# A gated-MLP and scan kernel: weights rounded by matmuls in two halves, statistics woven between other operations, prologue queues reordered

## What is computed

```python
x = L0_attn_x                                   # 4 x 1024 x 128, f32
xn = _layernorm(x)                              # over the last axis
x = x + attn(xn, ...) + ffn(xn, w_gate, w_up, w_down)

# attn: causal convolution of xn along time with a complex decaying phasor
#       plus the state carried in, times a gate, real part
# ffn:
def fp4_quant_dequant(x):                       # blocks of 16 along the last axis
    scale = max(max|xb| / 6, 1e-12)
    xn = xb / scale
    q = GRID[searchsorted(MID, |xn|)] * sign(xn) * scale   # grid 0 .5 1 1.5 2 3 4 6
def fp4_linear(x, w):
    return einsum('bsk,nk->bsn', fp4_quant_dequant(x), fp4_quant_dequant(w))
h = silu(fp4_linear(x, w_gate)) * fp4_linear(x, w_up)      # 352 wide
out = fp4_linear(h, w_down)
```

## Time and profile before

| what | us |
|---|---|
| median of 3 runs (range) | 137.78 (137.71 to 139.31) |
| the profiled execution, its own time | 136.63 |
| its span, first to last instruction | 134.8 |

### The profile page before, as it was taken

One profiled execution on the slowest core, in us unless ns is written; L12 is line 12 of the kernel. 1 busy time (PEld: TensorE's weight loads), 2 busy tenths in 40 slices (PEclk: granted clock), 3 DMA queues, 4 the chain that ended last, 5 costly groups with the idle time before them and its releaser, 6 DMA issues.

```text
span 134.8 us, 2143 instructions
## 1 busy us (share of the span) xinstructions
PE 111.7 (83%) x641; PEld 83.7 (62%) x641; DVE 120.6 (89%) x215; ACT 98.7 (73%) x223; POOL 110.4 (82%) x129
## 2 busy tenths in 40 slices
PE   3602789869376999899899999999999999976993
PEld 3501254536243877668786869587868878766882
DVE  0889999999999999979999999999999999899840
ACT  3869966699973899579897889579786648724631
POOL 4568996999699999999999999999999944982220
PEclk9985699986999999999999999999999999999999
DMA  4970000000000000200020020002000200100202
GB/s 125 359 301 9 0 2 0 0 5 0 0 0 0 5 0 0 78 0 0 0 83 0 0 75 12 0 0 78 0 0 0 83 0 0 55 22 5 78 0 80
DMA packets 2891, 4.90 MB, mean 36 GB/s; under 512 B 448, under 2 KB 832, under 8 KB 2880
## 3 DMA queue, kind: packets, MB, share of 16 engines
q1 hardware_dynamic: 2736, 4.77, 9.9%
q10 hardware_dynamic: 144, 0.00, 0.1%
HBM read 2.67 MB, written 2.10 MB: 35 GB/s over the span
## 4 chain that ended last, share of the span: by engine, by line
POOL 52%; issue 20%; PE 10%; DVE 7%; ACT 6%; DMA 2%; POOLq 1%; ACTq 0%
POOL hq L467 9%; POOL y_im L454 6%; POOL y_re L454 6%; POOL xt L411 6%; POOL xt L406 6%; POOL u_im L439 5%; POOL u_re L439 5%; POOL xv L401 3%; DMA par<-params_in 2%; PE ps_g L836 2%; POOL xv L416 2%; DVE bn L975 1%; ACT xbig L633 1%; PE ps_h L871 1%; PE ps_o L892 1%
## 5 line engine op out<-in xcount | busy, mean ns | idle before, releaser
L836 PE MATMUL ps_g<-wg_T,xq_T 128*128 128x352 f32 x64 | 26.6, 498 | 7.2 <-ACT silu L653 4.9
L467 POOL TENSOR_TENSOR hq<-hn,den 128x704 f32<-128x704 bf16 x15 | 20.8, 1387 | 4.3 <-DVE hn L1089 4.3
L892 PE MATMUL ps_o<-wd_T,hq_T 128*128 128x128 f32 x174 | 24.2, 275 | 0.0
L845 PE MATMUL ps_u<-wu_T,xq_T 128*128 128x352 f32 x64 | 22.9, 479 | 0.1
L892 PEld LDWEIGHTS ps_o<-wd_T,hq_T 128*128 128x128 f32 x174 | 22.1, 194 | 0.0
L653 ACT ACTIVATE silu<-ps_g 128x352 f32<-128x352 f32 x32 | 14.7, 461 | 8.4 <-PE ps_g L836 8.2
L659 ACT COPY hq_T<-ps_h 128x384 f32<-128x384 f32 x32 | 15.3, 479 | 5.3 <-PE ps_h L871 5.1
L836 PEld LDWEIGHTS ps_g<-wg_T,xq_T 128*128 128x128 f32 x64 | 10.3, 193 | 13.1 <-ACT silu L653 8.4
L663 ACT ACTIVATE big<-ps_u 128x704 bf16<-128x704 f32 (+1 forms) x17 | 12.2, 725 | 8.2 <-DVE ps_u L1077 8.1
L871 PE MATMUL ps_h<-ident,hq 128*128 128x128 f32 x96 | 16.1, 277 | 2.3 <-ACT hq_T L659 2.1
L871 PEld LDWEIGHTS ps_h<-ident,hq 128*128 128x128 f32 x96 | 11.5, 142 | 9.2 <-ACT hq_T L659 4.2
(11 more groups left out here) (172 smaller groups left out, 258.5 us busy)
## 6 DMA issues: line engine op xcount, KB each, us to landing
x_all<-x_in SPq DMA_DIRECT2D x8, 256.0 KB, 6.5
out<-x_all SPq DMA_DIRECT2D x7, 256.0 KB, 2.0
w_raw<-w_in SPq DMA_DIRECT2D x1, 560.0 KB, 6.2
out<-x_all SPq DMA_DIRECT2D x1, 128.0 KB, 2.1
out<-x_all SPq DMA_DIRECT2D x2, 64.0 KB, 1.6
par<-params_in ACTq DMA_DIRECT2D x1, 3.5 KB, 3.0
```

What stands on the lines that cost most here:

```text
L467: pool.tensor_tensor(hq_blocks(q), hn_blocks(q), pair_scales(den[q % 4]), ALU.mult).then_inc(s_hq, 1)
L836: pe.matmul(ps_g[:, 0:I], x_cols(t), wg_T[:, :], start=True, stop=True).then_inc(s_gate, 1)
L845: pe.matmul(slot(q)[:, j, 0:I], x_cols(t), wu_T[:, :], start=True, stop=True).then_inc(s_up, 1)
L892: m = pe.matmul(o, hq_T[t % 3][:, c * P:(c + 1) * P], wd_T[:, c, :], start=False, stop=(c == NCH - 1))
```

## The change

- **Gate and up weights.** DVE's two shifts of 768 columns go. ACT makes the big number in bf16 for each half of 384 columns (Square, then Identity: four operations in place of one Abs). PE copies the divided weights into PSUM (f32 identity matmul) and adds and subtracts the big number (bf16 matmuls with an identity and a negated identity) in the same accumulation. DVE then scales each half. The divided weights now lie in SBUF.
- **Down weights.** POOL's two shifts go; PE does the same with three matmuls (`round_down`), ACT copies the result out of PSUM, POOL scales it.
- **Statistics.** The Newton steps of groups 0 and 1 have single moments between them; those of groups 2 to 7 lie in front of and inside pair 0. All moments now stand ahead of pair 0.
- **Queues.** SP loads x2 ahead of w. POOL does `part_turns` one step earlier and no longer waits for the statistics; `divide_down` and `first_state` change place. ACT does sine ahead of the first normalisation, `decay_columns` early, the halves of w between the halves of x, `big_h(0)` ahead of `copy_in_table(1)`, `silu_tile(3)`, `copy_xnT(0)`, and `normalise(3)` behind `big_x(2)`. PE has 24 more warming transposes.

```diff
@@ sync
-                if g == HALVES:
+                if g == FIRST - 1:
                     sp.dma_start(w_raw[:, :], w_in[:, :]).then_inc(s_w, 16)
@@ gpsimd
-                    if n == 3:
+                    if n == 4:
                         part_turns()
...
             def part_turns():
                 pool.wait_ge(s_whole, 2)
-                pool.wait_ge(s_stats, 1)
...
-            def round_down():
-                pool.wait_ge(s_dbig, 1)
-                pool.tensor_tensor(wd_v[:, :], wd_big[:, :], wd_v[:, :], ALU.subtract).then_inc(s_dt, 1)
-                pool.wait_ge(s_dt, 1)
-                pool.tensor_tensor(wd_v[:, :], wd_big[:, :], wd_v[:, :], ALU.subtract).then_inc(s_dr, 1)
-                pool.wait_ge(s_dr, 1)
-                pool.tensor_tensor(blocks(w_q[:, GU:]), blocks(wd_v[:, :]), spread(w_scale[:, GU // BLK:]),
+            def scale_down():
+                pool.wait_ge(s_drc, 1)
+                pool.tensor_tensor(blocks(w_q[:, GU:]), blocks(wd_r[:, :]), spread(w_scale[:, GU // BLK:]),
                                    ALU.mult).then_inc(s_dq, 1)
@@ scalar
-            def abs_w():
+            def big_w(n):
+                cols = w_cols(n)
                 act.wait_ge(s_wv, 1)
-                act.activation(w_big[:, :], w_v, ACT.Abs, scale=K).then_inc(s_wabs, 1)
+                act.activation(w_sq[:, cols], w_v[:, cols], ACT.Square, scale=math.sqrt(BEND)).then_inc(s_wsq, 1)
+                act.wait_ge(s_wsq, n + 1)
+                act.activation(w_big[:, cols], w_sq[:, cols], ACT.Identity, bias=base_c).then_inc(s_wbig, 1)
...
+            def copy_rounded_down():
+                act.wait_ge(s_dr, 1)
+                act.copy(wd_r[:, :], ps_o[:, 0:I]).then_inc(s_drc, 1)
@@ tensor
+            def copy_w():
+                pe.wait_ge(s_wv, 1)
+                pe.wait_ge(s_dcol, 2 * PAIR)
+                for n in range(2):
+                    pe.matmul(w_bank(n), ident[:, :], w_v[:, w_cols(n)], start=True, stop=False)
+
+            def round_w(n):
+                pe.wait_ge(s_signs, 2)
+                pe.wait_ge(s_wbig, n + 1)
+                pe.matmul(w_bank(n), plus[:, :], w_big[:, w_cols(n)], start=False, stop=False)
+                pe.matmul(w_bank(n), minus[:, :], w_big[:, w_cols(n)], start=False, stop=True).then_inc(s_wr, 1)
...
             warm(ps_o, 16)
+            pe.wait_ge(s_diag, 3)
+            warm(ps_o, 24)
             in_table(0)
+            copy_w()
+            for n in range(2):
+                round_w(n)
             turn_weight(0)
@@ vector
-            def round_w():
-                dve.wait_ge(s_wabs, 1)
-                dve.scalar_tensor_tensor(w_v, w_big[:, :], FLOOR, w_v, ALU.max, ALU.subtract).then_inc(s_wstep, 1)
-                dve.wait_ge(s_wstep, 4)
-                dve.scalar_tensor_tensor(w_v, w_big[:, :], FLOOR, w_v, ALU.max, ALU.subtract).then_inc(s_wstep, 1)
-                dve.wait_ge(s_wstep, 5)
-                dve.tensor_tensor(blocks(w_q[:, 0:GU]), blocks(w_v), spread(w_scale[:, 0:GU // BLK]),
-                                  ALU.mult).then_inc(s_wq, 1)
+            def scale_w(n):
+                dve.wait_ge(s_wr, n + 1)
+                dve.tensor_tensor(blocks(w_q[:, w_cols(n)]), blocks(w_bank(n)),
+                                  spread(w_scale[:, n * NCH * XB:(n + 1) * NCH * XB]), ALU.mult).then_inc(s_wq, 1)
```

More of the change, by code:

```diff
@@ L259, in maxima, with sums @@
             return slot(q)[:, 0, I:I + HBP + XBG]
-        def sums(n, count):
-            bank = (ps_h, ps_o)[n]
-            return [bank[:, k * count:(k + 1) * count] for k in range(5)]
+        def sums(count):
+            return [ps_h[:, k * count:(k + 1) * count] for k in range(5)]
         def decay_row(q, j):
@@ L680, in copy_out @@
                 act.copy(flat(x_all[:, g * TG:(g + 1) * TG, :]), ps_o[:, :]).then_inc(s_oc, 1)
+            (n0, (a0, a1)), (n1, (b0, b1)) = enumerate(x_parts(0))
             whole_turns()
             diagonals()
+            sine()
             act.wait_ge(s_stats, 1)
             normalise(0, 0, TG)
[L686 removed]
+            cosine()
             normalise(1, 0, PAIR)
[L688 to L690 removed]
+            decay_columns()
+            big_x(0, n0, a0, a1)
+            big_w(0)
+            big_w(1)
+            big_x(0, n1, b0, b1)
+            copy_weight(0)
+            copy_xqT(0, n0, a0, a1)
+            copy_weight(1)
+            silu_tile(0)
             normalise(1, PAIR, TG)
+            silu_tile(1)
             copy_in_table(0)
[L693 to L699 removed]
+            copy_xqT(0, n1, b0, b1)
+            silu_tile(2)
             big_x(1, 1, 0, GT)
[L701 removed]
+            big_h(0, 0, 0, PAIR)
             copy_in_table(1)
@@ L932, in _ @@
                     turn_xn(q // 2 + 1)
+                if q == 0:
+                    round_down()
                 if q >= SETTLED and q % 2 == 0 and q + 1 < LAST:
@@ L1121, in scan_im @@
                 scan(g, q, 1, g_im, u_im, s_uim, s_gim, s_yim, first_im)
-            for q in range(SETTLED):
+            theta_step(0)
+            moments(0, 1)
+            theta_step(1)
+            moments(1, 2 * TG)
+            variance(0)
+            guess(0)
+            root(0, 0)
+            moments(8, 9)
+            root(0, 1)
+            root(0, 2)
+            root(0, 0)
+            moments(9, 10)
+            root(0, 1)
+            root(0, 2)
+            root(0, 0)
+            moments(10, 11)
+            root(0, 1)
+            root(0, 2)
+            moments(11, 12)
+            offset(0)
+            scale_of_w()
+            scale_of_first_x(0)
+            divide_w()
+            moments(12, 22)
+            scale_w(0)
+            moments(22, 24)
+            scale_w(1)
+            moments(24, NT)
+            variance(1)
+            guess(1)
+            first_x_amax(1)
+            root(1, 0)
+            first_x_scale(1)
+            root(1, 1)
+            first_x_inverse(1)
+            root(1, 2)
+            product(0)
+            root(1, 0)
+            amax_h(0)
+            root(1, 1)
+            scale_only(0, False)
+            root(1, 2)
+            inverse_only(0, False)
+            root(1, 0)
+            divide_h(0)
+            root(1, 1)
+            root(1, 2)
+            offset(1)
+            for q in range(1, SETTLED):
                 g = q // 2
-                if q > 0:
-                    shift_h(q - 1, 0, 0, PAIR)
-                    shift_back_h(q - 1, 0, 0, PAIR)
+                shift_h(q - 1, 0, 0, PAIR)
+                shift_back_h(q - 1, 0, 0, PAIR)
                 product(q)
```

178 lines of the change are left out of this document (100 added, 78 removed).

## The result

| | median us (range, runs) | profiled execution, its own time | its span |
|---|---|---|---|
| before, same chip | 137.75 (136.59 to 139.31, 4) | 136.63 | 134.8 |
| changed | 141.26 (140.87 to 142.01, 4) | 141.59 | 139.8 |

The ratio is 1.0277, 95% interval 1.022 to 1.0334: slower, by 3.5 us between the medians. The forecast was 138.7, range 135.4 to 141.0.

A forecast was written before the change was run, and what follows sets the result against it. The prediction took the end to hang on POOL's `shift_x(2)`, waiting for ACT's xbig(2). Sine, weights and ACT's queue behind `big_h(0)` delay it from 36.93 to 37.8; +0.9 on the median 137.78 gives 138.7, range 135.4 to 141.0.

The forecast's parts named there:

- Where the end hangs: The end moves with DVE's `shift_h(4)` at 58.97, and that one to one with POOL's `shift_x(2)` at 36.93.
- First step, sine: ACT's sine ahead of the first normalisation: first normalised tile at 10.28, x's maxima wait 0.87 us, 1.05 later than before.
- Second step, weights: Weights' way through ACT and PE: scalings at 17.35 and 18.41, product of pair 0 at 23.0 in place of 21.80.
- POOL's stall: POOL's `divide_x(0)`, due at 13.25, held by DVE's division of two SBUF operands until 14.1: 0.86 us.
- Third step, ACT behind `big_h(0)`: ACT takes 9.3 us, not 8.41, from `big_h(0)` to `big_h(1)`; `shift_x(2)` starts at 37.8, +0.9.
- The sum: End later by the +0.9 of `shift_x(2)`, DVE's slack not deciding.
- The clock rival: PE's clock falls ahead of the first gate tiles and ahead of `round_down`: together +2.8, 140.6; chance 0.22, shared with other costs.
- The count: The +0.9 added to the median of the kernel before, 137.78, to name 138.7.
- No stall: POOL's `divide_x(0)` isn't held, all from 14 us on 0.86 earlier: 137.8; chance 0.23 with small gains to -1.5.
- savings arrive: ACT quicker, so POOL's and DVE's saved work reaches `shift_x(2)`: -3.1, 134.7, or half, 136.3; chance 0.15.

The follow-up runs named there:

- experiment 6: Changed kernel with idle PE transposes: 14 ahead of xq(1)'s transposes, 28 behind the down weights' transposes, 16 in the last pair; 137.46 us, ratio 1.0007.
- 4: Changed kernel with 14 idle PE transposes ahead of xq(1)'s transposes and 28 behind the down weights' transposes; 139.12 us, ratio 1.0047.
- 12: Changed kernel with only the 28 idle PE transposes behind the down weights' transposes; 139.23 us, ratio 1.0077.
- 7: Experiment 6 with `silu_tile(6)` ahead of `normalise(3)` on ACT and 16 in place of 28 idle transposes; 138.71 us, ratio 1.0083.
- 8: Experiment 7 with the inverses of the gate and up weights' scales in PSUM; 137.80 us, ratio 1.0013.
- Experiment 2: Changed kernel with sine behind the first normalisation on ACT, as in the kernel before; 140.87 us, ratio 1.0206.
- experiment 10: Experiment 9 with sine behind the first normalisation on ACT; 136.44 us, ratio 0.9846.
- experiment 9: Experiment 6 with the inverses of the gate and up weights' scales in PSUM; 137.03 us, ratio 0.9969.
- experiment 3: Changed kernel with the inverses of the gate and up weights' scales in PSUM, so DVE's division reads one SBUF operand; 139.86 us, ratio 1.014.
- experiment 13: Kernel before with idle PE transposes in four places: 24 in the prologue, 10, 20 and 16 in its later waits; 137.78 us, ratio 0.9978.
- 14: Experiment 6 run again, beside the kernel before with idle transposes; 137.54 us, ratio 0.9991.

## Why the prediction was wrong, point by point

- **Where the end hangs.** Right in its first half: the end moves one to one with `shift_h(4)` (75.8 behind it, unless the tail is low). The claim that "the same operations in the same order in both kernels" lie behind `shift_x(2)` and that the two move one to one is the step that failed. It holds with PE high there (22.04 to 22.07 in nine traces) and not across levels: the changed kernel takes 24.62. The order wasn't the same either: `normalise(3)` now stood between xbig(2) and `silu_tile(6)`. That costs nothing by itself (22.05 in experiment 6, with the same order), but it makes PE's wait ahead of `gate_tile(7)` 3.88 us, where it was 2.78, and here the level fell behind it. I had priced ACT's list up to xbig(2) and stopped reading there. The cost is 2.6 us of the 5.0. That filling the wait keeps the level high is shown (experiments 4, 6 and 12); that the 1.1 us more is what brought it down is not, since the level fell in other traces behind shorter waits and stayed in one (7 and 8).
- **First step, sine.** Right: xn at 10.38 for 10.28, maxima at 12.05 after 0.87 idle; w was there. Experiment 2 confirms the 1 us at x's division; in its execution PE's low level took it back, while experiment 10 comes out 0.6 below 9 between the medians, 0.4 between the fastest runs.
- **Second step, weights.** Right: POOL's stall (0.86 forecast from 13.25; it came at 13.45 and 1.78 less 1.20 makes 0.6, experiment 3), the scalings at 17.36 and 18.42, the bf16 pair at about a third of a microsecond, product at 23.05. The pair in the trace:

```profile
16.84 0.32 PE L822 MATMUL ps_u<-w_big,plus 128*128 128x384 bf16 x1 [0.44 <-ACT w_big L614]
17.00 0.32 PE L823 MATMUL ps_u<-w_big,minus 128*128 128x384 bf16 x1
```

  They start 0.16 apart, which is what the Trainium skill ("TensorE: Matmul & The Clock Gate", Back-to-back issue gap) gives for 384 columns.
- **Third step, ACT behind `big_h(0)`.** Right as a schedule: with PE high, ACT takes 9.29 from `big_h(0)` to `big_h(1)` (26.32 to 35.61, experiment 6), against 9.3, and `shift_x(2)` starts at 37.71 to 37.78, against 37.8. In the changed kernel as it runs the same stretch of ACT takes 10.70, 1.4 us more, all of it waits for PE's low stretch at 30.3 to 33.7. The sum had that at nothing.
- **The clock rival.** It was nearest to the truth, with a chance of 0.22 that it shared with other costs. Of its two places one was met (low over the gate of tile 4 and `round_down`: 1.2 forecast, 1.4 measured, 1.65 in experiment 12); ahead of tile 1's gate the level stayed high; and the place that cost most, 40.6 to 47.4, wasn't in it. Its argument against itself, that the low stretch of before lay over the same matmuls and was paid already, was wrong: experiment 13 shows that the stretch of before cost 0.0 at `shift_x(2)`. There ACT's silu came 0.2 earlier without it (31.71 for 31.90), and ACT then waited 0.26 for DVE's division ahead of `big_h(1)`, at 34.83 in both. I priced a level by the matmuls under it, where the price is the wait of whoever is next behind them.
- **The count.** The sum +0.9 was added to the median of before, 137.78, which is 1.2 above its fastest run; what the slower ones meet no trace shows. Between the fastest runs the sum fits: 136.45 and 137.34.
- **No stall, and savings arrive.** Both fell: the stall was there, and DVE's and POOL's savings (2.5 and 1.8 us of busy time) went into waits.

The parts of the 5.0 us. The profiled executions do not begin alike: DVE's first operation waits for the load of the parameters, which comes at 3.83 in the changed kernel, 3.66 in experiment 6, 3.75 before. The row of the changed kernel, then that of experiment 6:

```profile
3.83 0.16 DVE L1008 TENSOR_TENSOR vec<-par 128x1 f32<-128x1 f32 x1 [3.83 <-DMA par<-params_in]
...
3.66 0.16 DVE L1016 TENSOR_TENSOR vec<-par 128x1 f32<-128x1 f32 x1 [3.66 <-DMA par<-params_in]
```

Counted from there, `shift_x(2)` is at 33.18 before (33.21 in experiment 13), at 34.05 in 6 (34.06 in 4) and at 35.50 in the changed kernel. So of the profiled 5.0 us, 0.1 is the later start, 0.9 the change's own order, 1.4 the first low stretch and 2.6 the second (24.62 less 22.05). Experiment 10 stands at 33.21: with the inverses in PSUM and sine behind the normalisation the own order's 0.9 is gone. What stays open: why the level falls in one execution and not in another of the same kernel; and whether the kernel before, with its tail and its prologue held high in each execution, would come under the 136.44 of experiment 10. Its fastest, 136.45, is equal to that.

## What to carry to other kernels

Where an engine's work is moved, follow the engine that feeds TensorE through the whole stretch that changed, and list TensorE's idle time there as a cost of its own: some microseconds in which it waits can halve its clock for the next, and the loss is set by who waits for those matmuls. Before judging such a change, run both versions with idle transposes in TensorE's holes and compare the traces where the level was high in both; the difference that is left is the schedule's, and here it was 0.9 of the 5.0 us. The medians did not show it, as the transposes did not keep the level high in every execution. A kernel whose runs spread by some per cent may be meeting low stretches in some executions: two versions that keep TensorE busy ran within 0.6 us (experiment 6) and 0.4 us (10) where the kernel before spread over 5 us, though others still spread over 1.3 (9) to 3.2 us (13).

## What the runs showed of the hardware

- The same program has its low stretches at other places in other executions. Experiments 6 and 14 are one program: in 6 the prologue's 24 transposes take 5.38 us and the first two table matmuls behind them 1.29, in 14 they take 2.84 and 1.87. The Trainium skill ("TensorE: Matmul & The Clock Gate", Part 1: The HAM clock gate) says too that the cold matmuls differ in number from run to run, and the two traces agree. It puts the penalty of the first ramp to the high level at under 1% of a typical kernel's span. That figure isn't meant for falls in mid-kernel: what the idle transposes took away here was 3.8 us of 141.3, 2.7%.
- The granted clock shown ahead of its first change in a trace cannot be relied on. The 24 transposes in the prologue read 1.00 in the changed kernel and take 5.38 us; in experiment 9 they read 1.00 as well and take 2.84. The durations tell the level:

```profile
7.75 5.38 PE L811 MATMUL ps_o<-ident 128*128 128x128 f32 x24 [2.03 <-ACT diag L573]
```

- Idle transposes are cheap where PE waits anyway: the block of 28 lasts 3.22 us in experiment 6, and the gate matmul behind it still waits 0.82 us for ACT.
